# One comparison a tile for both kinds of one-hots, and attention's denominators turned, guarded on GpSimd and spread by a product

## The chip, the cores and the metric

One core of a Trainium2 chip runs the kernel. The metric is the device time of one execution in microseconds (us). Three runs of the kernel before gave 431.22, 433.67 and 428.87 us.

## The reference, cut to what matters

One layer of a graph transformer on 3125 nodes with 256 features. `xn` is the layer norm of x. The graph part sums, for every node, the rows of `xn` over its 53125 edges, adds `w * xn`, and passes the sum through three small products. The mixing part is linear attention over all nodes with 8 heads of 32 features: with q and k after `elu + 1`,

```
k_sum   = k.sum(nodes)                                  # per head, 32 numbers
D_inv   = 1 / maximum(q . k_sum, 1e-6)                  # per node and head
context = k^T v                                         # per head, 32 x 32
attn    = (q @ context) * D_inv
x = x + graph(xn) + attn @ Wproj^T + bproj
x = x + moe(layernorm(x))                               # 8 experts, the best 2 of each token
```

The denominator of one node and head is the product of that node's 32 q features with the head's `k_sum`; its guarded inverse multiplies all 32 features of that head.

## The kernel before, in words

The nodes lie in 25 tiles of 125. The kernel has four stages: projections (q, k, the graph's first product), then the counting stage, which holds all of the change, then routing, then 62 chunks of expert work.

**Counts.** The graph sum is made as a product with a matrix of edge counts. For one tile of 125 nodes, the 625 groups of 5 destination nodes are taken 25 at a time, each with a window of 128 sorted edges on the 128 partitions. VectorE makes two one-hots of every window: `koh` (which of the 125 sources' positions, 126 wide, `key_onehots`, L986) and `loh` (which of 125 places, 128 wide, `local_onehots`, L992), 25 of each, in two instructions of 3150 and 3200 bf16 elements per partition. TensorE multiplies them, 25 products a tile in 7 groups (`count_chunks`, L1366, products at L1381). ScalarE copies each group out (`store_chunks`, L725), two DMA transposes turn the tile's counts (L442, L450), and TensorE multiplies them with the graph's features (`add_up`, L1425, products at L1432, and the node's own term at L1422). Both one-hots are double buffered: VectorE waits for all counts of tile t-2 before it writes those of tile t.

**Attention.** While tile t+1 is counted, tile t is attended to, in a ring over three engines. `denominators(t)` (L1452) multiplies the q features of the tile, as the stationary operand (128 by 125), with `ksum_of` (128 by 8), which gives 125 nodes by 8 heads, in two fp32 products. VectorE (`invert`, L1048) takes the maximum with 1e-6 (L1056) and then the reciprocal (L1057) on 125 by 8. GpSimd (L605) copies each inverse 32 times side by side, to 125 by 256. TensorE (`spread`, L1458) turns that in two transposes (L1463) into features by nodes and runs the next tile's `denominators` right behind. VectorE multiplies with q (`divide`, L1087), TensorE multiplies with the mixing matrix (`attend`, L1475), and VectorE adds the result to x (`mix_add`, L1094).

**Order.** Each engine's program is written out by hand and run in order. TensorE's loop for t = 1 to 24 counts tile t+1 in 7 groups, with `attend(t-1)` after groups 1 and 2, `spread(t)` after group 3 (group 4 for t = 1) and `add_up(t-1)` after group 5. VectorE's loop (L1097) is: both one-hots of t+2, `divide(t)`, `invert(t+1)`, `mix_add(t-1)`; for t = 0 it makes no one-hots and adds nothing, and for t = 1 the one-hots of tile 3 come right behind `invert(1)`. GpSimd has nothing else to do in this stage. SyncE issues the DMA transposes.

**Before the stage.** GpSimd fills constants at the start (L489 to L524). `make_keys` (L955) writes the keys and places that the one-hots are compared with, each doubled, to two separate arrays of 625 by 2.

Of the kernel before, what the change touches and what calls it, by code (L numbers as in the profile page):

```python
# [6 lines left out]
F32, F16, BF16 = mybir.dt.float32, mybir.dt.float16, mybir.dt.bfloat16  # L7
# [17 lines left out]
EPS = 1e-5  # L25
MAGIC = 12582912.0
CB = 2 * TP
ROW = D + 6
# [36 lines left out]
def build(nc, a, out):  # L65
# [4 lines left out]
    with ExitStack() as ctx:  # L70
# [45 lines left out]
        def homes(region, at, n):  # L116
# [18 lines left out]

        r = Region("region_a", GT * (KW + P) + 2 * NT * P + 2)
        koh = r.take(P, 2 * GT * KW, BF16).rearrange("p (s c n) -> p s c n", s=2, c=GT)
        loh = r.take(P, 2 * GT * P, BF16).rearrange("p (s c n) -> p s c n", s=2, c=GT)
        adj = [r.take(P, NT * P, BF16).rearrange("p (t n) -> p t n", t=NT) for _ in range(2)]
        r.take(P, 2)  # L140
        adjT_at = r.at
# [8 lines left out]
        assert r.at <= adjT_at + NT * P  # L150
        r.restart(adjT_at - 2 - NT * P // 2)
        eq = r.take(P, 4 * TP).rearrange("p (s n) -> p s n", s=2)
        rq = r.take(P, 4 * TP).rearrange("p (s n) -> p s n", s=2)
        assert r.at <= adjT_at - 2
        r.restart()
# [100 lines left out]
        spill = sb("spill", [P, 1], I32)  # L256
        keys = sb("keys", [P, NG, 2], BF16)
        locs = sb("locs", [P, NG, 2], BF16)

# [3 lines left out]
        ksum_of = sb("ksum_of", [P, 2, NH])  # L263
        den = sb("den", [TP, 2, 2 * NH])
        wide = sb("wide", [TP, 2, D])
        qn = sb("qn", [P, 2, 2 * TP])
# [50 lines left out]
            "value_done", "held_done", "held_ready", "turned", "keys_done", "spill_known"))  # L317
        pad_zeroed, wident_done, koh_done, loh_done, chunk_ready, adj_done = map(sem, (
            "pad_zeroed", "wident_done", "koh_done", "loh_done", "chunk_ready", "adj_done"))
# [3 lines left out]
        den_ready, den_inv, widened, den_spread, qn_done, mix_ready, mix_added = map(sem, (  # L323
            "den_ready", "den_inv", "widened", "den_spread", "qn_done", "mix_ready", "mix_added"))
        spill_copied, spill_landed, spill_step, spill_ready, spill_summed = map(sem, (
# [162 lines left out]
        def _(pool):  # L488
# [34 lines left out]
            nc.gpsimd.tensor_copy(ident16[:], ident[:]).then_inc(pool_set, 1)  # L523
            nc.gpsimd.memset(adj[0][:, :, TP:P], 0.0).then_inc(pad_zeroed, 1)  # L524

            def set_tables():
# [73 lines left out]
            for t in range(NT):  # L600
                pool.wait_ge(den_inv, t + 1)
                if t >= 2:
                    pool.wait_ge(den_spread, t - 1)
                heads = den[:, 1, t % 2 * NH:(t % 2 + 1) * NH].rearrange("p (h a) -> p h a", a=1)
# [248 lines left out]
        def _(dve):  # L853
# [101 lines left out]
            def make_keys(second):  # L955
                if not second:
# [9 lines left out]
                link(nc.vector.tensor_scalar(keyf[:, lo:hi], keyf[:, lo:hi], MAGIC, -MAGIC, ALU.add, ALU.add))  # L966
                twice = keyf[:, lo:hi].rearrange("p (n a) -> p n a", a=1).to_broadcast([P, n, 2])
                nc.vector.scalar_tensor_tensor(
                    locs[:, lo:hi, :], twice, -float(P),
                    got.rearrange("p (n a) -> p n a", a=1).to_broadcast([P, n, 2]), ALU.mult, ALU.add)  # L970
                nc.vector.tensor_scalar(keys[:, lo:hi, :], twice, unheld[:, 0:1], None, ALU.add
                                        ).then_inc(keys_done, 1)
# [5 lines left out]

            def columns(v, t, n):
                return v[:, t * GT:(t + 1) * GT, :].rearrange("p c (a u) -> p c a u", a=1).to_broadcast(  # L980
                    [P, GT, n // 2, 2])

            def counting(n):
                return iota16[:, 0:n].rearrange("p (a m u) -> p a m u", a=1, u=2).to_broadcast([P, GT, n // 2, 2])

            def key_onehots(t):  # L986
                if t >= 2:
                    dve.wait_ge(chunk_ready, NBLK * (t - 1))
                nc.vector.tensor_tensor(koh[:, t % 2, :, :].rearrange("p c (m u) -> p c m u", u=2), counting(KW),  # L989
                                        columns(keys, t, KW), ALU.is_equal).then_inc(koh_done, 1)  # L990

            def local_onehots(t):  # L992
                if t >= 2:
                    dve.wait_ge(chunk_ready, NBLK * (t - 1))
                nc.vector.tensor_tensor(loh[:, t % 2, :, :].rearrange("p c (m u) -> p c m u", u=2), counting(P),  # L995
                                        columns(locs, t, P), ALU.is_equal).then_inc(loh_done, 1)

            link(moments(0, J, 0))
# [5 lines left out]
            for t in range(NT):  # L1004
# [32 lines left out]
                if t in (17, 18):  # L1037
                    make_keys(t == 18)
                if t == 19:
                    key_onehots(0)  # L1040
                if t == 20:
                    local_onehots(0)
                if t == 21:
                    key_onehots(1)
                if t == 22:
                    local_onehots(1)

            def invert(t):  # L1048
                if t == 0:
                    dve.wait_ge(den_ready, 1)  # L1050
                else:
                    dve.wait_ge(den_spread, t)
                if t >= 2:
                    dve.wait_ge(widened, t - 1)
                heads = slice(t % 2 * NH, (t % 2 + 1) * NH)
# [16 lines left out]
            last.then_inc(ksum_done, 1)  # L1072
            key_onehots(2)
# [3 lines left out]
            local_onehots(2)  # L1077
            dve.wait_ge(heads_ready, 1)
# [235 lines left out]
        def _(pe):  # L1314
# [51 lines left out]
            def count_chunks(n):  # L1366
                t, i = divmod(n, NBLK)
                lo, hi = BLOCKS[i]
                if i == 0:
                    pe.wait_ge(koh_done, t + 1)  # L1370
                    pe.wait_ge(loh_done, t + 1)
                if n == 0:
                    pe.wait_ge(keys_done, 2)
                elif n < NBLK:
                    pe.wait_ge(adj_done, n)
                elif n > 2 * NBLK:
                    pe.wait_ge(adj_done, n - 2)
                elif n > NBLK:
                    pe.wait_ge(adj_done, n - 1)
                for c in range(lo, hi):  # L1380
                    last = nc.tensor.matmul(count_bank(n)[:, (c - lo) * TP:(c - lo + 1) * TP], loh[:, t % 2, c, :],  # L1381
                                            koh[:, t % 2, c, 0:TP], start=True, stop=True)
                last.then_inc(chunk_ready, 1)
# [352 lines left out]
```

## Time and profile before

| | |
|---|---|
| runs | 428.87, 431.22, 433.67 us |
| profiled execution, its own time | 430.48 us |
| its span, first to last instruction | 428.8 us |
| mean granted TensorE clock, share of full speed | 0.962 |
| TensorE busy with products | 404.5 us, 94% |
| VectorE busy | 311.2 us, 73% |
| ScalarE busy | 265.8 us, 62% |
| GpSimd busy | 183.5 us, 43% |

The 1.68 us between the span and the execution's own time lie around the first and the last instruction. PE is TensorE's products and PEld its weight loads, DVE is VectorE, ACT ScalarE, POOL GpSimd, and SPq SyncE's queue of DMAs. Busy shares are means over four stages with different limits; the counting stage is the stretch from about 97 to 220 us. An fp32 product stands in the trace as two passes, and a row says "x4" for two products. The chain of waits is the work that ended last, followed back from the end; each piece is counted from the end of the piece before it, so its pieces can be added, while the durations in the timeline include latency and overlap.

### The profile page before, as it was taken

The numbers are of one execution on the slowest core, as the hardware profiler recorded it, in microseconds if no ns is written. First come the engines' busy times: TensorE is split into PE (matmuls) and PEld (weight loads), VectorE is DVE, ScalarE is ACT, GpSimd is POOL, SyncE is SP. The second block draws the span as 40 slices with busy tenths as digits, with TensorE's granted clock in tenths as the row PEclk, the third lists the DMA queues.
The fourth block names the chain that finished last, engine by engine and source line by source line (L and its number), as shares of the span: only waits on it lengthen the run. The fifth ranks groups of instructions, "written<-read, shape, count | busy, mean of one in ns | idle before, by whom it ended". The sixth has DMA issues, their size and how long they took to land.

```text
span 428.8 us, 10052 instructions
## 1 busy us (share of the span) xinstructions
PE 404.5 (94%) x3141; PEld 318.8 (74%) x3141; DVE 311.2 (73%) x785; ACT 265.8 (62%) x676; POOL 183.5 (43%) x298
## 2 busy tenths in 40 slices
PE   4989899997999999999999999978999999999995
PEld 1767678776677777777755667854999998988894
DVE  3688858967899999999727653667688887655553
ACT  1756655575788888888824614441776766666663
POOL 4058969246100010001091114464456565655655
PEclk9899999999999999999999987577999999999999
DMA  8927310006589999999997961124465665467651
GB/s 211 194 70 255 90 26 8 1 2 125 106 152 172 172 175 167 179 184 189 167 215 227 308 224 63 65 81 120 151 190 188 187 210 159 140 202 207 186 177 38
DMA packets 111827, 64.11 MB, mean 150 GB/s; under 512 B 87985, under 2 KB 102202, under 8 KB 111646
## 3 DMA queue, kind: packets, MB, share of 16 engines
q1 hardware_dynamic: 104590, 48.14, 51.0%
q0 software_dynamic: 6368, 14.47, 9.6%
q10 hardware_dynamic: 816, 0.85, 0.8%
q8 instruction: 26, 0.43, 0.4%
q14 instruction: 27, 0.22, 0.2%
HBM read 24.00 MB, written 21.44 MB: 106 GB/s over the span
## 4 chain that ended last, share of the span: by engine, by line
PE 52%; POOL 12%; issue 11%; DMA 10%; DVE 10%; ACT 3%; SPq 1%; POOLq 0%; DVEq 0%
PE bank L1432 9%; PE bank L1381 8%; PE bank L1475 6%; POOL xs_next L653 5%; PE bank L1346 4%; PE bank L1444 4%; DMA region_a<-xs_next 4%; PE bank L1355 3%; POOL out L660 3%; DMA out<-region_a 3%; PE bank L1612 2%; PE bank L1594 2%; PE bank L1454 2%; DMA xs_next<-region_a 2%; POOL region_a L648 2%
## 5 line engine op out<-in xcount | busy, mean ns | idle before, releaser
L725 ACT CAST region_a<-bank 128x500 bf16<-128x500 f32 (+1 forms) x119 | 70.0, 673 | 14.8 <-PE bank L1381 14.8
L1681 PE MATMUL bank<-region_a,region_c 128*128 128x128 f32 x496 | 65.6, 275 | 0.0
L1692 PE MATMUL bank<-region_c,region_a 128*128 128x256 f32 x248 | 64.0, 380 | 0.0
L1681 PEld LDWEIGHTS bank<-region_a,region_c 128*128 128x128 f32 x496 | 60.3, 191 | 0.1
L1142 DVE COPY region_c<-region_w 128x1026 f32 x62 | 43.5, 701 | 19.2 <-issue 17.7
L605 POOL COPY wide<-den 125x256 f32<-125x256 f32 x25 | 13.0, 518 | 100.6 <-DVE den L1057 100.6
L1381 PE MATMUL bank<-region_a 128*128 128x125 bf16 x625 | 52.9, 219 | 1.5 <-ACT region_a L725 1.4
L1381 PEld LDWEIGHTS bank<-region_a 128*128 128x128 bf16 x625 | 42.2, 101 | 13.6 <-ACT region_a L725 3.2
L989 DVE TENSOR_TENSOR region_a<-iota,keys 128x3150 bf16<-128x3150 bf16 x25 | 44.9, 1796 | 5.4 <-PE bank L1381 5.4
L1304 DVE SCALAR_TENSOR_TENSOR region_a<-bank,region_a 128x256 f32<-128x256 f32 x62 | 30.0, 484 | 22.1 <-PE bank L1692 19.9
L815 ACT COPY region_a<-bank 128x256 f32<-128x256 f32 x62 | 23.1, 373 | 36.9 <-PE bank L1670 36.8
L995 DVE TENSOR_TENSOR region_a<-iota,locs 128x3200 bf16<-128x3200 bf16 x25 | 45.9, 1835 | 0.0
L1692 PEld LDWEIGHTS bank<-region_c,region_a 128*128 128x128 f32 x248 | 42.3, 191 | 3.7 <-ACT region_a L823 0.3
L653 POOL DMA_INDIRECT xs_next<-region_a x31 | 31.0, 999 | 29.1 <-POOL region_a L648 22.9
L634 POOL DMA_INDIRECT xs<-rows,slot_i x25 | 24.7, 987 | 43.8 <-ACT rows L769 28.3
L1432 PE MATMUL bank<-region_a,region_z 125*64 125x500 bf16 (+1 forms) x375 | 40.7, 347 | 0.0
L660 POOL DMA_INDIRECT out<-region_a x31 | 30.6, 986 | 23.1 <-POOL region_a L648 15.5
L823 ACT ACTIVATE region_a<-bank,region_c 128x128 f32<-128x128 f32 x124 | 38.5, 362 | 0.0
L725 ACT CAST region_w<-bank 128x500 bf16<-128x500 f32 (+1 forms) x56 | 32.4, 667 | 9.0 <-PE bank L1381 9.0
L1432 PEld LDWEIGHTS bank<-region_a,region_z 125*64 125x64 bf16 x375 | 21.8, 109 | 17.4 <-DMA region_a<-region_w 0.2
L834 ACT COPY bank<-region_q 128x256 f32 x62 | 23.4, 377 | 18.3 <-DVE region_a L1304 16.4
L1346 PE MATMUL bank<-region_p,region_a 128*125 128x320 f32 x100 | 32.2, 445 | 0.0
(239 smaller groups left out, 775.6 us busy)
## 6 DMA issues: line engine op xcount, KB each, us to landing
region_a<-xs_next SPq DMA_DIRECT2D x31, 259.0 KB, 2.9
region_w<-in_w SPq DMA_DIRECT2D x4, 1024.0 KB, 9.7
region_a<-xs SPq DMA_DIRECT2D x31, 131.0 KB, 2.4
rows<-in_x SPq DMA_DIRECT2D x5, 560.0 KB
xs_next<-null SPq DMA_DIRECT2D x8, 259.0 KB, 4.9
xs_next<-null SPq DMA_DIRECT2D x1, 1554.0 KB, 11.4
xs<-null SPq DMA_DIRECT2D x8, 131.0 KB, 3.1
region_q<-in_b SPq DMA_DIRECT2D x1, 1024.0 KB, 9.6
```

Source lines behind the costliest of these rows:

```text
L653: nc.gpsimd.indirect_dma_start(xs_next, bass.IndirectOffsetOnAxis(to_row[:, c:c + 1], 0), xch[:, c % XB, :], None, bounds_check=RR - 1, oo ...
L660: nc.gpsimd.indirect_dma_start(out, bass.IndirectOffsetOnAxis(to_row[:, c:c + 1], 0), xch[:, c % XB, PART:WIDE], None, bounds_check=N - 1, ...
L725: nc.scalar.copy(to, count_bank(n)[:, 0:w * TP].rearrange("p (c t u) -> p c t u", c=w, t=NT)).then_inc(adj_done, 1)
L823: last = nc.scalar.activation(hT[:, c % 2, f * P:(f + 1) * P], hid_ps[c % 2][:, f * P:(f + 1) * P], ACT.Gelu, bias=wc[:, c % 3, 4 * D + f: ...
L989: nc.vector.tensor_tensor(koh[:, t % 2, :, :].rearrange("p c (m u) -> p c m u", u=2), counting(KW), columns(keys, t, KW), ALU.is_equal).th ...
L995: nc.vector.tensor_tensor(loh[:, t % 2, :, :].rearrange("p c (m u) -> p c m u", u=2), counting(P), columns(locs, t, P), ALU.is_equal).then ...
L1142: nc.vector.tensor_copy(wc[:, c % 3, :].rearrange("p (a f) -> p a f", a=1), w_all[:, bass.ds(e, 1), :]).then_inc(w_copied, 1)
L1346: last = nc.tensor.matmul((y0, y1)[s][0:TP, 0:H1 + D], xnT[:, s, k, :], wzkv[:, k, 0:H1 + D], start=(k == 0), stop=(k == 1))
L1381: last = nc.tensor.matmul(count_bank(n)[:, (c - lo) * TP:(c - lo + 1) * TP], loh[:, t % 2, c, :], koh[:, t % 2, c, 0:TP], start=True, stop ...
L1432: last = nc.tensor.matmul(sum_out(lo, hi - lo), zparts[:, t, part, :], adjT[0:TP, t % 2, lo:hi, 0:TP], start=False, stop=False, skip_group ...
L1681: last = nc.tensor.matmul(hid_ps[c % 2][:, f * P:(f + 1) * P], wc[:, c % 3, k * D + f * P:k * D + (f + 1) * P], xT[:, c % 2, k * P:(k + 1) ...
L1692: last = nc.tensor.matmul(y_ps[c % 2][:, 0:D], hT[:, c % 2, f * P:(f + 1) * P], wc[:, c % 3, (2 + f) * D:(3 + f) * D], start=False, stop=( ...
```

## The change

VectorE makes both one-hots of a tile with one instruction of 6300 elements: the array `onehots` holds them as kinds 0 and 1, each in rows of 128, of which 126 are written; the last two columns of kind 1 are set to zero once, as VectorE's first instruction. Tiles 0 to 2 keep two instructions, one for each kind. The keys and places stand interleaved by tile in `pairs`, so one operand reaches both.

The denominators of a tile come out as 8 heads by 125 nodes: `ksum_of` is now the stationary operand and q the moving one. VectorE takes the reciprocal straight from PSUM, 8 partitions by 125 elements. GpSimd applies the guard as a minimum with 1e6 on the same shape. A product with `head_of` (8 by 256, one where the feature belongs to the head) spreads the inverse over the features, in place of the copy and the two transposes. `head_of` is made by GpSimd at the start with a memset and two selects.

```diff
+        onehots = r.take(P, 4 * GT * P, BF16).rearrange("p (s k c n) -> p s k c n", s=2, k=2, c=GT)
-        den_ps = h0[0:TP, CB:CB + NH]
+        den_ps = h0[0:NH, CB:CB + TP]
...
+            nc.gpsimd.memset(head_of[:], 1.0).then_inc(pool_set, 1)
+            nc.gpsimd.affine_select(out=head_of[:], ...)          # twice
...
-                pool.wait_ge(den_inv, t + 1)
+                pool.wait_ge(inverted, t + 1)
                 if t >= 2:
                     pool.wait_ge(den_spread, t - 1)
-                nc.gpsimd.tensor_copy(wide[:, t % 2, :].rearrange("p (h a) -> p h a", a=HD),
-                                      heads.to_broadcast([TP, NH, HD])).then_inc(widened, 1)
+                nc.gpsimd.tensor_scalar(den[:, 1, t % 2, :], den[:, 0, t % 2, :], 1.0 / DEN_MIN, None, ALU.min
+                                        ).then_inc(den_inv, 1)
...
-            def key_onehots(t): ...
-            def local_onehots(t): ...
+            def make_onehots(t, kinds):
+                if t >= 2:
+                    dve.wait_ge(chunk_ready, NBLK * (t - 1))
+                n = len(kinds) * GT
+                kinds = slice(kinds[0], kinds[-1] + 1)
+                return nc.vector.tensor_tensor(
+                    onehots[:, t % 2, kinds, :, 0:KW].rearrange("p k c (m u) -> p (k c) m u", u=2),
+                    iota16[:, 0:KW].rearrange("p (a m u) -> p a m u", a=1, u=2).to_broadcast([P, n, KW // 2, 2]),
+                    pairs[:, t, kinds, :, :].rearrange("p k c (a u) -> p (k c) a u", a=1).to_broadcast([P, n, KW // 2, 2]),
+                    ALU.is_equal)
+            nc.vector.memset(onehots[:, :, 1, :, KW:P], 0.0)
...
             def invert(t):
...
-                link(nc.vector.tensor_scalar(den[:, 0, heads], den_ps, 1e-6, None, ALU.max))
-                nc.vector.reciprocal(den[:, 1, heads], den[:, 0, heads]).then_inc(den_inv, 1)
+                nc.vector.reciprocal(den[:, 0, t % 2, :], den_ps).then_inc(inverted, 1)
...
                 if 1 <= t < NT - 2:
-                    key_onehots(t + 2)
-                    local_onehots(t + 2)
+                    make_onehots(t + 2, (0, 1)).then_inc(onehots_done, 1)
...
             def denominators(t):
                 for c in range(2):
-                    last = nc.tensor.matmul(den_ps[:, 0:NH], qp_all[:, t, c * TP:(c + 1) * TP], ksum_of[:, c, :],
+                    last = nc.tensor.matmul(den_ps, ksum_of[:, c, :], qp_all[:, t, c * TP:(c + 1) * TP],
                                             start=(c == 0), stop=(c == 1))
             def spread(t):
-                pe.wait_ge(widened, t + 1)
+                pe.wait_ge(den_inv, t + 1)
...
-                    last = nc.tensor.transpose(spread_ps[:, c * TP:(c + 1) * TP], wide[:, t % 2, c * P:(c + 1) * P],
-                                               ident[0:TP, 0:TP])
+                    last = nc.tensor.matmul(spread_ps[:, c * TP:(c + 1) * TP], head_of[:, c * P:(c + 1) * P],
+                                            den[:, 1, t % 2, :], start=True, stop=True)
```

## Rows read from the trace of the kernel before

**Rows 1.** Busy us, 150 to 180: TensorE, loads, VectorE, ScalarE, GpSimd; clock, DMA, GB/s.
```profile
150.00:180.00 30.00, 30.00 (x338) 22.83 (x335) 28.23 (x42) 25.32 (x46) 2.80 (x7) 1.00 1.05 180
```

**Rows 2.** Chain of waits, whole run: start, us, what; `add_up` of four tiles.
```profile
115.69 1.56 PE bank L1432 x15
...
149.58 1.45 PE bank L1432 x13
...
191.85 1.56 PE bank L1432 x15
...
215.00 1.56 PE bank L1432 x15
```

**Rows 3.** Chain of waits, one tile from 157.9 us: what TensorE does in turn.
```profile
157.91 0.22 PE bank L1463 x2
158.13 0.34 PE bank L1454 x4
...
160.54 0.62 PE bank L1381 x9
...
161.65 0.23 PE bank L1381 x4
```

**Rows 4.** Chain of waits, projections: eight fp32 passes of 125 columns.
```profile
51.39 0.90 PE bank L1355 x8
```

**Rows 5.** Timeline of one tile: start, us, engine, line, shapes, idle before.
```profile
156.06 1.80 DVE L989 TENSOR_TENSOR region_a<-iota,keys 128x3150 bf16<-128x3150 bf16 x1 [0.22 <-PE bank L1381]
...
157.78 1.82 DVE L995 TENSOR_TENSOR region_a<-iota,locs 128x3200 bf16<-128x3200 bf16 x1
...
159.51 0.41 DVE L1087 TENSOR_TENSOR qn<-bank,region_q 128x250 f32<-128x250 f32 x1
159.84 0.16 DVE L1056 TENSOR_SCALAR den<-bank 125x8 f32<-125x8 f32 x1
...
160.04 0.20 DVE L1057 RECIPROCAL den<-den 125x8 f32<-125x8 f32 x1
...
160.30 0.40 POOL L605 COPY wide<-den 125x256 f32<-125x256 f32 x1 [4.28 <-DVE den L1057]
...
160.74 1.80 DVE L989 TENSOR_TENSOR region_a<-iota,keys 128x3150 bf16<-128x3150 bf16 x1 [0.22 <-PE bank L1381]
...
162.42 0.39 PE L1463 MATMUL bank<-ident,wide 125*128 125x125 f32 x2
```

**Rows 6.** VectorE's groups by shape: busy us, mean ns, idle; two widths of reciprocal.
```profile
L873 DVE RECIPROCAL rstd<-std 125x10 f32<-125x10 f32 x2 | 0.4, 214 | 0.0
...
L1180 DVE RECIPROCAL rstd<-std 125x3 f32<-125x3 f32 x2 | 0.4, 176 | 0.4 <-ACT std L766 0.4
```

**Rows 7.** Timeline of the stage's start, 102 to 109 us: the ring's first two rounds.
```profile
102.68 0.15 DVE L1056 TENSOR_SCALAR den<-bank 125x8 f32<-125x8 f32 x1
...
102.98 1.77 DVE L995 TENSOR_TENSOR region_a<-iota,locs 128x3200 bf16<-128x3200 bf16 x1
103.13 1.89 POOL L605 COPY wide<-den 125x256 f32<-125x256 f32 x1 [0.89 <-DVE den L1057]
...
105.88 0.42 DVE L1087 TENSOR_TENSOR qn<-bank,region_q 128x250 f32<-128x250 f32 x1 [0.72 <-PE bank L1454]
...
106.67 1.86 POOL L605 COPY wide<-den 125x256 f32<-125x256 f32 x1 [1.66 <-DVE den L1057]
...
108.19 2.02 DVE L995 TENSOR_TENSOR region_a<-iota,locs 128x3200 bf16<-128x3200 bf16 x1
...
108.58 0.43 PE L1463 MATMUL bank<-ident,wide 125*128 125x125 f32 x2 [0.67 <-POOL wide L605]
```

**Rows 8.** Timeline of the kernel's start: first instructions after the constants.
```profile
6.49 1.73 DVE L865 BATCH_NORM_STATS2 stats<-rows 125x6 f32<-125x256 f32 x5 [6.49 <-DMA rows<-in_x]
...
10.14 1.36 POOL L552 TENSOR_SCALAR rows<-rows,rstd,shift 125x256 f32<-125x256 f32 x2 [5.18 <-DVE region_a L882]
```

**Rows 9.** VectorE's groups by shape: the keys of four fifths of the tiles.
```profile
L971 DVE TENSOR_SCALAR keys<-region_c,unheld 128x1000 bf16<-128x1000 f32 x1 | 0.7, 735 | 0.0
```

More of the change, by code:

```diff
@@ L26 @@
 MAGIC = 12582912.0
+DEN_MIN = 1e-6
 CB = 2 * TP
@@ L134, in build @@
         zr = sb("zr", [TP, J, H1])[:]
-        r = Region("region_a", GT * (KW + P) + 2 * NT * P + 2)
-        koh = r.take(P, 2 * GT * KW, BF16).rearrange("p (s c n) -> p s c n", s=2, c=GT)
-        loh = r.take(P, 2 * GT * P, BF16).rearrange("p (s c n) -> p s c n", s=2, c=GT)
+        r = Region("region_a", 2 * GT * P + 2 * NT * P)
+        onehots = r.take(P, 4 * GT * P, BF16).rearrange("p (s k c n) -> p s k c n", s=2, k=2, c=GT)
         adj = [r.take(P, NT * P, BF16).rearrange("p (t n) -> p t n", t=NT) for _ in range(2)]
-        r.take(P, 2)
         adjT_at = r.at
@@ L256, in build @@
         spill = sb("spill", [P, 1], I32)
-        keys = sb("keys", [P, NG, 2], BF16)
-        locs = sb("locs", [P, NG, 2], BF16)
+        pairs = sb("pairs", [P, NB * 5, 2, GT, 2], BF16)
+        keys, locs = pairs[:, :, 0, :, :], pairs[:, :, 1, :, :]
         mout = sb("mout", [P, 2, D])
@@ L263, in build @@
         ksum_of = sb("ksum_of", [P, 2, NH])
-        den = sb("den", [TP, 2, 2 * NH])
-        wide = sb("wide", [TP, 2, D])
+        den = sb("den", [NH, 2, 2, TP])
+        head_of = sb("head_of", [NH, D])
         qn = sb("qn", [P, 2, 2 * TP])
@@ L524, in _ @@
             nc.gpsimd.memset(adj[0][:, :, TP:P], 0.0).then_inc(pad_zeroed, 1)
+            nc.gpsimd.memset(head_of[:], 1.0).then_inc(pool_set, 1)
+            pool.wait_ge(pool_set, 3)
+            nc.gpsimd.affine_select(out=head_of[:], in_=head_of[:], compare_op=ALU.is_ge, fill=0.0, base=0,
+                                    pattern=[[1, D]], channel_multiplier=-HD).then_inc(pool_set, 1)
+            pool.wait_ge(pool_set, 4)
+            nc.gpsimd.affine_select(out=head_of[:], in_=head_of[:], compare_op=ALU.is_ge, fill=0.0, base=HD - 1,
+                                    pattern=[[-1, D]], channel_multiplier=HD).then_inc(pool_set, 1)
             def set_tables():
@@ L966, in make_keys @@
                 link(nc.vector.tensor_scalar(keyf[:, lo:hi], keyf[:, lo:hi], MAGIC, -MAGIC, ALU.add, ALU.add))
-                twice = keyf[:, lo:hi].rearrange("p (n a) -> p n a", a=1).to_broadcast([P, n, 2])
+                tiles = slice(lo // GT, hi // GT)
+                by_tile = "p (t c a) -> p t c a"
+                twice = keyf[:, lo:hi].rearrange(by_tile, c=GT, a=1).to_broadcast([P, n // GT, GT, 2])
                 nc.vector.scalar_tensor_tensor(
-                    locs[:, lo:hi, :], twice, -float(P),
-                    got.rearrange("p (n a) -> p n a", a=1).to_broadcast([P, n, 2]), ALU.mult, ALU.add)
-                nc.vector.tensor_scalar(keys[:, lo:hi, :], twice, unheld[:, 0:1], None, ALU.add
+                    locs[:, tiles, :, :], twice, -float(P),
+                    got.rearrange(by_tile, c=GT, a=1).to_broadcast([P, n // GT, GT, 2]), ALU.mult, ALU.add)
+                nc.vector.tensor_scalar(keys[:, tiles, :, :], twice, unheld[:, 0:1], None, ALU.add
                                         ).then_inc(keys_done, 1)
@@ L977, in make_keys @@
                                             ).then_inc(wident_done, 1)
[L979 to L986, printed above, removed]
+            def make_onehots(t, kinds):
                 if t >= 2:
                     dve.wait_ge(chunk_ready, NBLK * (t - 1))
[L989 to L996, printed above, removed]
+                n = len(kinds) * GT
[6 more added lines that the diff above has]
+            nc.vector.memset(onehots[:, :, 1, :, KW:P], 0.0)
             link(moments(0, J, 0))
@@ L1038, in _ @@
                     make_keys(t == 18)
[L1039 to L1046, printed above, removed]
+                if t in (19, 21):
+                    make_onehots((t - 19) // 2, (0,))
+                if t in (20, 22):
+                    make_onehots((t - 20) // 2, (1,)).then_inc(onehots_done, 1)
             def invert(t):
@@ L1053, in invert @@
                 if t >= 2:
-                    dve.wait_ge(widened, t - 1)
-                heads = slice(t % 2 * NH, (t % 2 + 1) * NH)
-                link(nc.vector.tensor_scalar(den[:, 0, heads], den_ps, 1e-6, None, ALU.max))
-                nc.vector.reciprocal(den[:, 1, heads], den[:, 0, heads]).then_inc(den_inv, 1)
+                    dve.wait_ge(den_inv, t - 1)
+                nc.vector.reciprocal(den[:, 0, t % 2, :], den_ps).then_inc(inverted, 1)
             dve.wait_ge(ctx_ready, 1)
@@ L1072, in _ @@
             last.then_inc(ksum_done, 1)
-            key_onehots(2)
+            make_onehots(2, (0,))
             dve.wait_ge(ctx_turned, 1)
@@ L1076, in _ @@
             invert(0)
-            local_onehots(2)
+            make_onehots(2, (1,)).then_inc(onehots_done, 1)
             dve.wait_ge(heads_ready, 1)
@@ L1380, in count_chunks @@
                 for c in range(lo, hi):
-                    last = nc.tensor.matmul(count_bank(n)[:, (c - lo) * TP:(c - lo + 1) * TP], loh[:, t % 2, c, :],
-                                            koh[:, t % 2, c, 0:TP], start=True, stop=True)
+                    last = nc.tensor.matmul(count_bank(n)[:, (c - lo) * TP:(c - lo + 1) * TP], onehots[:, t % 2, 1, c, :],
+                                            onehots[:, t % 2, 0, c, 0:TP], start=True, stop=True)
                 last.then_inc(chunk_ready, 1)
```

16 lines of the change are left out of this document (7 added, 9 removed).

## The prediction

> **What bounds the kernel now.** I read the busy times by stretch first. In the counting stage TensorE is busy for all of 30 us at full granted clock, VectorE for 28.2 of them [rows 1]. Busy products alone prove nothing, so the chain of waits comes next: there the same product line returns tile after tile, and its distance changes with TensorE's work and with nothing else. Seven tiles in a row take (149.58 - 115.69)/7 = 4.84 us, five later ones (215.00 - 191.85)/5 = 4.63 us [rows 2]. The first seven run the node's own fp32 product by itself, the last five have none. A loop that another engine paced would not notice. Over all 21 tiles between the first and the last row the mean is 99.31/21 = 4.73 us. Third, the timeline of one tile: VectorE goes round in 3.45 us of one-hots (156.06 to 159.51), 0.33 to the maximum, 0.20 to the reciprocal and 0.48 to the end of the addition, 4.46 us, and then stands 0.22 us idle until TensorE has finished a count [rows 5]. So TensorE sets the pace and VectorE follows closely. What the change saves on VectorE and GpSimd is worth nothing until TensorE is shorter; what it adds to TensorE is paid every tile.
>
> **TensorE, every tile.** Before, the two transposes take 0.22 us and the two denominator products 0.34 us, 0.56 in all [rows 3]. The transposes are one pass each, and the denominators pass only 8 columns. After, both are full fp32 products with 125 moving columns: two for `spread`, two for the denominators, eight passes. The nearest row is the projection of q, also fp32, 125 columns and 128-column weights: eight passes in 0.90 us, 0.11 each [rows 4]. The bounds: at the price of a bf16 count of 125 columns, 0.23/4 = 0.058 us [rows 3], eight passes cost 0.46, a gain of 0.10; from above, 0.11 plus a change of array shape, priced below. I take 0.90, the row with the same type and width: **+0.34 us a tile**. The pace becomes 4.97 to 5.18 us, 5.07 in the mean. Rounds 2 to 24 of `spread` and the 22 denominators behind them pay it: 22 x 0.34 + (0.45 - 0.22) = **+7.7 us**.
>
> **VectorE, every tile.** The merged one-hots take between 3.30 us (3.45 less one small instruction, 0.15) and the old 3.45; I take 3.40, since nearly all elements remain. The maximum and its wait, 0.20, go. The reciprocal grows from 8 columns to 125, on fewer partitions. No row shows that width. Three columns take 176 ns and ten take 214 [rows 6], 5.4 ns a column, so 125 take 0.214 + 115 x 0.0054 = 0.84 us. From below the bound is the present 0.20 us; from above a price with no fixed part, 0.20/8 x 125 = 3.1 us, which the seven columns for 38 ns speak against. The round is then 3.40 + 0.33 + 0.84 + 0.28 = 4.85 us. That is 0.39 longer than now, yet hidden under TensorE's 4.97; the cover is only 0.12 us.
>
> **GpSimd, every tile.** The minimum covers 125 elements where the copy wrote 256 in 0.40 us; I take 0.3, between 0.15 and 0.40. It starts 0.06 us behind the reciprocal, beside the addition, and has until the next one-hots: 0.28 us of addition and 0.12 or more of idle time. TensorE asks for it 1.68 us after the one-hots begin [rows 5]. Hidden.
>
> **The stage's start, once.** Here the ring is bare, and GpSimd's copy runs beside one-hots: it takes 1.89 and 1.86 us in place of 0.40, and comes out 0.26 us after the one-hot instruction that began just before it [rows 7]. The Trainium skill's "SBUF — State Buffer" (the part on engine ports) says the pair of ports that the two engines share is locked for a whole instruction; the two rows agree. In the second round the copy slips out between the two one-hot instructions. Merged, there is no gap. Step by step:
> - Reciprocal from 102.68 to 103.52, one-hots until 105.21, guard out 105.47 (the copy: 105.02).
> - `spread(0)`, then `divide(0)`: 0.86 us after the copy before, now 1.20 with the 0.34, so 106.67 (105.88 before).
> - Reciprocal 107.00 to 107.84; merged one-hots 107.76 to 111.21; guard out 111.47. The copy was out at 108.53, and TensorE had already been waiting 0.67 us for it: 2.94 us late, all of it idle.
> - `spread(1)` with its products: 0.34 more.
>
> **+3.3 us.** In the third round `mix_add` waits for TensorE, and the guard slips in. Bounds: with a reciprocal of 0.20 and eight passes at 0.46, the same steps give +1.1; with a reciprocal of 1.15, +3.9.
>
> **What costs nothing.** The Vector queue's new memset stands ahead of statistics that wait 6.49 us for x; GpSimd's memset and two selects fall into 5.18 us of waiting before its first row scaling [rows 8]. The keys are written in another arrangement with as many elements; one such instruction takes 0.735 us [rows 9], and I take 0 for it, with 0.7 as the upper end. No DMA is added or moved.
>
> **Sum.** 430.48 + 7.7 + 3.3 = **441.5 us**. The profiled execution is 0.7 under the median of the runs shown, so against that median the same sum would be 442.2; I forecast 441.5, and 437 to 445 as this case's own range.
>
> **Rivals.**
> - *VectorE becomes the pace.* From a reciprocal of 0.96 us on, its round is longer than TensorE's shortest tile. With a slope half as steep again as the row's, 8.1 ns, it takes 0.214 + 115 x 0.0081 = 1.15 us and the round 5.16: 21 x 5.16 - 99.31 = 9.1, plus 3.9 at the start and 0.6 for the last rounds, **444.1 us**. Against it: the slope of rows 6. For it: the cover is 0.12 us. 
> - *The array's shape is changed more often.* Behind the 64-column products, nine counts take 0.62 us, while nine at 0.058 are 0.52 [rows 3]: a change costs about 0.10. Operands 8 wide could add two changes a tile, 23 x 0.20 = 4.6: **446.1 us**. The Trainium skill's "TensorEngine Tiling (Array Packing)" (key properties) says that a change of tiling mode drains the engine; whether 8 rows or 8 columns make one, no row shows.
> - *The guard is shut out by the one-hots in the steady state.* If GpSimd loses the 0.4 us window, it comes out some 0.2 after 3.45 us of one-hots, and TensorE, which asks at 1.68, stands 2.0 us. VectorE then idles behind TensorE and the next guard slips through, so every second tile pays: 11 x 2.0 on top, **463.5 us**. It decides once the guard has not begun when the addition ends. Against it: at 108.19 the one-hots were stretched to 2.02 us while GpSimd finished [rows 7], so the engine that begins first keeps its turn.
> - *Narrow operands make fp32 passes cheap, and it is not slower.* If a pass with 8 rows or 8 columns in use costs what a bf16 count of 125 columns does, 0.058 us, each tile gains 0.10: -2.3 us, and the start costs 2.4: **430.6 us**. Break-even for the tile is 0.07 a pass. Against it: the q projection at 0.11, and the own product, whose two passes make 4.84 of 4.63, 0.11 each, with half of the columns [rows 2, 4]. To be clearly faster it would also need the start to cost nothing.
>
> **How the numbers follow.** Chances: forecast 0.58, VectorE 0.15, array shape 0.10, shut-out 0.04, not slower 0.13, of which 0.04 falls below -1%. A measurement of this kernel can tell about 1%, 4.3 us, from no change. All cases but the last are slower by more than that, less 0.01 for a forecast that comes out small: slower 0.86, same 0.10, faster 0.04. The range takes in the forecast with its bounds (start +1.1, keys 0.7, passes), VectorE and array shape: 435 to 449 us, 0.83 of the chance.
>
> **What would show it.** TensorE still without idle time between 120 and 210 us, `add_up` returning every 5.07 us, and the two products together at 0.9 us in the chain: right. A reciprocal near 0.84 us, and VectorE idle before the one-hots by 0.1 to 0.3 us: the cover held. TensorE idle in every tile, released by the one-hots, is the first rival; by GpSimd's guard in every second tile, the third. TensorE waiting some 3 us at `spread(1)` shows the start. If passes with 8 rows take under 0.07 us, the prediction is wrong at its main term.

## The result, and the profile after

The kernel after takes **452.64 us** (median of 4 runs, 450.94 to 456.70) against 430.38 for the kernel before, a ratio of **1.0532** [1.0485, 1.0579]. Slower was right; 441.5 was not, nor the range to 449. The profiled execution takes 453.56 us with a span of 451.8, so it stands 23.08 above that of before.

First, where in the span it lies: the chain of waits of the kernel after (start, us, what). L1455 is `spread`, L1446 `denominators`, L1373 the counts, L1424 `add_up`.

```profile
112.72 1.22 PE bank L1455 x4
...
115.40 2.95 PE bank L1424 x15
...
124.20 1.56 PE bank L1424 x15
...
160.95 0.63 PE bank L1455 x4
161.58 0.53 PE bank L1446 x4
162.11 0.55 PE bank L1373 x8
162.65 1.45 PE bank L1424 x13
...
164.26 0.60 PE bank L1373 x9
...
165.35 0.22 PE bank L1373 x4
...
167.98 1.45 PE bank L1424 x13
...
237.15 1.56 PE bank L1424 x15
...
239.21 6.40 DMA region_a<-region_a
...
245.65 1.63 PE bank L1424 x15
```

`add_up(1)`, at 115.69 before, starts at 124.20: **+8.5 us**. One tile's price is in this number, since `spread(2)` and its products stand ahead of `add_up(1)` in TensorE's program. From there to `add_up(22)`, 21 tiles take 237.15 - 124.20 = 112.95 us, where they took 99.31 [rows 2]: **+13.6**, or 5.38 us a tile for 4.73. The last `add_up` of the kernel before, in its chain:

```profile
222.40 1.44 PE bank L1432 x15
```

From `add_up(22)` to there the last two rounds took 7.40 us, now 8.50: **+1.1**; 0.4 of it is the last `spread`, the rest TensorE's wait for a DMA transpose at the end. Behind that nothing is lost: 451.8 - 245.65 = 206.15 us against 428.8 - 222.40 = 206.4. The three terms make 23.2.

Inside a tile, against [rows 3]: `spread` 0.63 for 0.22, `denominators` 0.53 for 0.34, and the eight counts behind them 0.55, where eight at the 0.058 of [rows 3] are 0.46. That is 0.41 + 0.19 + 0.09 = 0.69. The other counts are slightly cheaper (0.60 for 0.62, 0.22 for 0.23), and the distance from `add_up` to `add_up` grows from 4.68 to 5.33, by 0.65.

Is TensorE still the pace? The windows of the kernel after (stretch: busy us and count of TensorE, loads, VectorE, ScalarE, GpSimd; granted clock, DMA share, GB/s):

```profile
104.00:105.00 1.00, 0.02 (x1) 0.00 (x0) 1.00 (x1) 0.00 (x0) 1.00 (x1) 1.00 0.05 11
105.00:106.00 1.00, 0.24 (x2) 0.24 (x3) 0.70 (x3) 0.00 (x0) 0.70 (x1) 1.00 1.10 213
106.00:108.00 2.00, 2.00 (x12) 1.22 (x12) 0.26 (x1) 0.00 (x0) 0.00 (x0) 0.50 1.13 216
...
118.00:119.00 1.00, 1.00 (x9) 0.68 (x7) 0.00 (x0) 0.00 (x0) 0.00 (x0) 0.50 0.00 0
...
120.00:122.00 2.00, 1.83 (x18) 1.39 (x17) 1.67 (x2) 1.45 (x3) 0.00 (x0) 1.00 0.81 154
...
150.00:180.00 30.00, 30.00 (x303) 20.99 (x303) 27.45 (x24) 22.00 (x39) 2.75 (x6) 1.00 0.93 159
```

From 150 to 180 us TensorE is busy throughout, as in [rows 1], and VectorE less than before. The upper rows show what the forecast had no term for: TensorE is nearly idle from 104 to 106 us, and the granted clock then stands at 0.50, its level of 1.2 GHz, until 119 us. In the kernel before TensorE is busy for 0.93 us between 104 and 106, and the clock stays at 1.00.

The timeline of the kernel after for one tile and for the second round of the start (start, us, engine, line, shapes, idle time before):

```profile
103.75 1.95 POOL L610 TENSOR_SCALAR den<-den 8x125 f32<-8x125 f32 x1 [1.45 <-DVE den L1051]
...
105.76 1.02 PE L1455 MATMUL bank<-den,head_of 8*128 8x125 f32 x4 [1.74 <-POOL den L610]
...
108.93 3.36 DVE L991 TENSOR_TENSOR region_a<-iota,pairs 128x6300 bf16<-128x6300 bf16 x1
109.09 3.58 POOL L610 TENSOR_SCALAR den<-den 8x125 f32<-8x125 f32 x1 [3.39 <-DVE den L1051]
...
162.82 0.92 DVE L1051 RECIPROCAL den<-bank 8x125 f32<-8x125 f32 x1
...
163.83 0.51 POOL L610 TENSOR_SCALAR den<-den 8x125 f32<-8x125 f32 x1 [4.99 <-DVE den L1051]
...
164.46 3.44 DVE L991 TENSOR_TENSOR region_a<-iota,pairs 128x6300 bf16<-128x6300 bf16 x1 [0.45 <-PE bank L1373]
```

TensorE waits 1.74 us for the first guard. In the steady state VectorE waits 0.45 us for TensorE, and the guard finishes within the addition and that wait. At the start the guard stands beside the merged one-hots for 3.58 us and comes out 0.38 us behind them.

### The profile page after: what moved, and what is told of

It is laid out like the page before. It is cut to its first block, busy times and chain, and to the rows that moved or that the text cites. A ratio compares the mean times of both kernels' runs of the same rounds, so it can differ in the third digit from the quotient of the medians.

```text
span 451.8 us, 10105 instructions
## 1 busy us (share of the span) xinstructions
PE 422.6 (94%) x3187; PEld 324.4 (72%) x3191; DVE 322.6 (71%) x739; ACT 265.3 (59%) x676; POOL 189.2 (42%) x301
## 4 chain that ended last, share of the span: by engine, by line
PE 54%; DVE 21%; DMA 8%; issue 7%; ACT 4%; SPq 2%; DVEq 2%; POOL 2%; POOLq 0%; ACTq 0%
PE bank L1424 8%; PE bank L1373 8%; PE bank L1467 5%; DVE region_c L1135 4%; PE bank L1339 4%; PE bank L1455 3%; PE bank L1436 3%; PE bank L1673 3%; PE bank L1684 3%; PE bank L1446 3%; PE bank L1348 3%; DVE region_a L1297 3%; PE bank L1604 2%; DVE region_a L1291 2%; DMA out<-region_a 2%
## 5 line engine op out<-in xcount | busy, mean ns | idle before, releaser
L991 DVE TENSOR_TENSOR region_a<-iota,pairs 128x6300 bf16<-128x6300 bf16 (+1 forms) x28 | 86.5, 3090 | 10.0 <-PE bank L1373 10.0
L730 ACT CAST region_a<-bank 128x500 bf16<-128x500 f32 (+1 forms) x119 | 69.0, 662 | 25.8 <-PE bank L1373 25.7
L610 POOL TENSOR_SCALAR den<-den 8x125 f32<-8x125 f32 x25 | 17.3, 692 | 118.9 <-DVE den L1051 118.9
L1373 PE MATMUL bank<-region_a 128*128 128x125 bf16 x625 | 53.5, 222 | 1.4 <-ACT region_a L730 1.4
L1373 PEld LDWEIGHTS bank<-region_a 128*128 128x128 bf16 x625 | 40.3, 99 | 19.5 <-ACT region_a L730 6.3
L1297 DVE SCALAR_TENSOR_TENSOR region_a<-bank,region_a 128x256 f32<-128x256 f32 x62 | 30.0, 484 | 23.2 <-PE bank L1684 20.7
L820 ACT COPY region_a<-bank 128x256 f32<-128x256 f32 x62 | 23.2, 374 | 37.5 <-PE bank L1662 37.2
L1424 PE MATMUL bank<-region_a,region_z 125*64 125x500 bf16 (+1 forms) x375 | 42.1, 356 | 0.7 <-DMA region_a<-region_a 0.7
L1424 PEld LDWEIGHTS bank<-region_a,region_z 125*64 125x64 bf16 x375 | 22.2, 112 | 19.3 <-issue 1.6
L1467 PE MATMUL bank<-mout,qn 128*125 128x256 f32 x100 | 32.2, 409 | 0.2 <-DVE rows L1088 0.2
```

The lines of the kernel that those rows point to most:

```text
L730: nc.scalar.copy(to, count_bank(n)[:, 0:w * TP].rearrange("p (c t u) -> p c t u", c=w, t=NT)).then_inc(adj_done, 1)
L991: return nc.vector.tensor_tensor(onehots[:, t % 2, kinds, :, 0:KW].rearrange("p k c (m u) -> p (k c) m u", u=2), iota16[:, 0:KW].rearrange ...
L1297: nc.vector.scalar_tensor_tensor(xch[:, s, PART:WIDE], y_ps[c % 2][:, 0:D], xch[:, s, weight:weight + 1], xch[:, s, PART:WIDE], ALU.mult, ...
L1424: last = nc.tensor.matmul(sum_out(lo, hi - lo), zparts[:, t, part, :], adjT[0:TP, t % 2, lo:hi, 0:TP], start=False, stop=False, skip_group ...
L1467: last = nc.tensor.matmul(mix_ps[0:TP, 0:D], qn[:, t % 2, c * TP:(c + 1) * TP], mout[:, c, :], start=(c == 0), stop=(c == 1))
```

## The experiments

Theory A: the narrow operands cost TensorE a price at each change of shape, and the start costs a late guard and the clock that falls. Rivals: narrow fp32 passes are slower in themselves; VectorE or GpSimd sets the pace. Changes stand against the kernel after unless said otherwise. Ratios are against the kernel before. "Start" is the place of `add_up(1)`, less the shift of the whole stage in that execution (read at the copy of `mout`, 102.08 us before and 102.13 after). Outside the counting stage the profiled executions differ also between kernels that are the same there: in the fourteen profiles the copy of `mout` starts between 102.03 and 105.01 us, and from the last `add_up` to the end 203.1 to 208.7 us pass, with the granted clock below 1.00 for a part of that in every one. So a step is priced inside the stage, and medians of four runs tell small steps less well.

**1. Full width for both products.**

```diff
-        den = sb("den", [NH, 2, 2, TP])
-        head_of = sb("head_of", [NH, D])
-        ksum_of = sb("ksum_of", [P, 2, NH])
+        den = sb("den", [P, 2, 2, TP])          # rows from 8 on are zero
+        head_of = sb("head_of", [P, D])         # as above
+        ksum_of = sb("ksum_of", [P, 2, P])      # columns from 8 on are zero
...
```

> The changed kernel with both narrow operands filled up with zeros: head_of and the guarded inverses on 128 rows in place of 8, ksum_of 128 columns in place of 8. The same products, the same number of moving columns. Theory A (operands 8 wide cost extra, by a change of the array's shape): spread falls from 0.64 to about 0.45 us, denominators from 0.53 to about 0.45, the counts behind them from 0.55 to 0.47: the pace falls by 0.25 to 0.35 us a tile to about 5.0 to 5.05, 446 to 448 us. Theory B (fp32 products in this place cost what they cost, whatever their width): pace unchanged at 5.3 to 5.5, 452 to 453 us.

444.69 us, 1.0324 [1.0243, 1.0405], a little below what was expected. The chain of this kernel, its first and last of 22 `add_up` and one tile (the lines stand one further down than after):

```profile
122.28 1.56 PE bank L1425 x15
...
162.10 0.50 PE bank L1456 x4
162.60 0.45 PE bank L1447 x4
163.05 0.44 PE bank L1374 x8
...
228.49 1.56 PE bank L1425 x15
```

The same eight passes with sixteen times the rows or columns are **cheaper**: 0.13, 0.08 and 0.11 us less, 0.32 a tile. The 21 tiles take 106.21 us, 5.06 each; the forecast's pace was 5.07. The +0.34 was thus the price of full-width operands, and the change doesn't have these.

**2. Full width for `spread` alone** (the first two lines above).

> The changed kernel with only the spreading product filled up, 128 rows in place of 8; the denominators keep their 8 columns. Theory A: spread 0.64 to about 0.45 us, denominators stay 0.53; pace 5.1 to 5.15, 448 to 450 us. Theory B: nothing moves, 452 to 453 us. If the extra sits in the change between the two shapes and not in either product, it comes out between the two or shifts to the denominators.

448.92 us, 1.0416 [1.0334, 1.0499]. The chain:

```profile
165.08 0.50 PE bank L1456 x4
165.58 0.53 PE bank L1447 x4
166.11 0.55 PE bank L1374 x8
```

One excess goes, that of `spread`; those of the denominators and of the counts stay.

**3 and 4. Each pair of narrow products issued twice**, `spread`'s or the denominators', into the same place.

```diff
-                    last = nc.tensor.matmul(spread_ps[...], head_of[...], den[...], start=True, stop=True)
+                    for _ in range(2):
+                        last = nc.tensor.matmul(spread_ps[...], head_of[...], den[...], start=True, stop=True)
```

> The kernel after with the two products of spread issued twice, one pair behind the other, into the same place. It tells the two halves of the narrow operands' price apart. Theory A (a fixed price of about 0.10 us each time the products change their shape: full to 8 rows, 8 rows to 8 columns, 8 columns to full): the repeated pair changes no shape once it has begun, since its weights alternate between two 8-row blocks, so it costs the full-width price of four passes, 0.45 to 0.50 us a tile; pace 5.33 to 5.80, time 452.6 + 22 x 0.47 = 463. Theory B (an fp32 pass with 8 rows is itself slower, 0.16 us in place of 0.11): the repeated pair costs 0.63 a tile; pace 5.96, time 466.5.

> The kernel after with the two denominator products issued twice. Theory A (a fixed price at each change of shape): the repeated pair costs 0.42 to 0.46 us a tile, the pace goes from 5.33 to about 5.77 and the time to about 462. Theory B (a pass into 8 columns is itself slower): 0.53 a tile, pace 5.86, time 464.

460.72 us (1.0756 [1.0720, 1.0792]) and 462.58 us (1.0779 [1.0742, 1.0816]). The chain with `spread` twice:

```profile
162.74 1.08 PE bank L1456 x8
163.82 0.52 PE bank L1446 x4
```

The chain with the denominators twice (L1449 are the repeated ones):

```profile
165.11 0.63 PE bank L1458 x4
165.74 0.53 PE bank L1446 x4
166.27 0.43 PE bank L1449 x4
```

The second `spread` costs 1.08 - 0.63 = 0.45 us and the second denominators 0.43: four passes at 0.11, the price of [rows 4]. Narrow passes are therefore not slower in themselves; what costs is the first group after each change, from full to 8 rows, to 8 columns, and back to full. That settles it for the rival "slow passes". With `spread` twice the time came out 2 us below the expectation; the start of its profiled execution is 0.9 us earlier than after's, which is a part of that.

**5. The guard on VectorE instead of GpSimd.**

```diff
-                nc.gpsimd.tensor_scalar(den[:, 1, t % 2, :], den[:, 0, t % 2, :], 1.0 / DEN_MIN, None, ALU.min)
+                nc.vector.tensor_scalar(den[:, 1, t % 2, :], den[:, 0, t % 2, :], 1.0 / DEN_MIN, None, ALU.min)
...                                         # the waits move with it
```

> The changed kernel with the guard (the minimum on 8 by 125) on VectorE, right behind the reciprocal, in place of GpSimd. Theory: in the steady tiles nothing moves, since VectorE idles 0.45 us a tile and the guard costs it about 0.2: pace stays 5.33 to 5.49 us. At the start the guard no longer waits out one-hots (1.95 and 3.58 us on GpSimd), spread(1) comes 3 to 5 us earlier, TensorE has no long idle time and the granted clock stays at 2.4 GHz: 6 to 8 us less, 444.5 to 447 us. Rival (the start's delay is the wider products and the reciprocal, not GpSimd's wait): less than 2 us, over 450.5 us. Rival 2 (VectorE is the hidden pace): the pace grows by 0.2 us a tile, 4 us lost again.

448.12 us, 1.0412 [1.0351, 1.0473], above the expectation. The chain of this kernel, first three `add_up`:

```profile
109.24 1.56 PE bank L1421 x15
...
116.00 1.56 PE bank L1421 x15
...
121.49 1.56 PE bank L1421 x15
```

The pace is unchanged (5.49 us here, 5.33 later). The start is back at 116.00 (115.69 before), and the clock stays at 1.00 in it: nearly the whole +8.5 hangs on the guard's place on GpSimd. By the medians that is worth 4.5 us, not 8.2; this profiled execution spends 2 us more than after's behind the stage, at work that the edit leaves alone.

**6. The clock held at the start:** products of zeros keep TensorE busy where it waited.

```diff
+            filler(8)                # 8 products of zeros, added to a bank of sums
             spread(0)
...
+                    if t == 1 and i == 4:
+                        filler(11)
```

> The changed kernel with 8 products of zeros in front of spread(0) and 11 in front of spread(1), 512 columns each, added to a bank that is being summed, so TensorE is busy where it waited for GpSimd. Theory C (the start costs 8.5 us, of which some 4 to 6 because the granted clock falls to 1.2 GHz from 106 to 119 us): the clock stays at 2.4 GHz there, and the time falls by 4 to 6 us to 447 to 449; add_up of tile 1 comes at about 119 to 120 in place of 124.2 us. Rival D (the late guard alone makes the start, the clock is beside the point): the clock stays up and the time falls by less than 1.5 us. Rival E: products of zeros don't keep the clock, nothing changes.

450.57 us, 1.0484 [1.0392, 1.0576], less gained than expected. The windows of this kernel:

```profile
106.00:108.00 2.00, 1.99 (x13) 1.02 (x12) 0.74 (x3) 0.00 (x0) 0.74 (x1) 1.00 1.11 213
...
114.00:116.00 2.00, 2.00 (x23) 1.10 (x21) 1.26 (x2) 0.72 (x1) 0.35 (x1) 1.00 0.00 0
```

and its chain, the second guard and the first two `add_up`:

```profile
109.41 3.59 POOL den L610
...
114.60 1.56 PE bank L1424 x15
...
121.36 1.56 PE bank L1424 x15
```

The clock stays at 1.00. `add_up(1)` starts at 121.36, in an execution whose stage began 1.09 us later than before (`mout` at 103.17): +4.6. So of the +8.5 in after's profile 3.9 us are the clock. By the medians it is 2.1, whose interval takes in zero. In the other kernels that keep the late guard, the stretch at half clock has other lengths (about 109 to 112 us with the denominators twice), so one execution's 3.9 us is no constant.

**7. Full width and the guard on VectorE** (1 and 5 together): what is left, and who sets the pace.

> Both narrow operands filled up to the whole array and the guard on VectorE: the best mended form of the changed ring. TensorE's work is 5.0 us a tile; VectorE's is about 4.9 plus the guard's 0.2. Theory: VectorE now sets the pace at 5.05 to 5.15 us, TensorE waits 0.05 to 0.15 us a tile for one-hots, the start is 6 us shorter than in the changed kernel: 437 to 441 us, still 1.5 to 2.5% over the kernel before, since spread and denominators cost 0.95 us against 0.56. Rival (the two repairs don't add, because the start's clock was already better with the filled operands): 442 to 444 us.

441.02 us, 1.0205 [1.0133, 1.0277]. Its windows:

```profile
150.00:180.00 30.00, 30.00 (x320) 23.05 (x318) 29.80 (x31) 23.39 (x43) 0.00 (x0) 1.00 0.95 165
```

and its timeline of VectorE:

```profile
158.88 3.42 DVE L988 TENSOR_TENSOR region_a<-iota,pairs 128x6300 bf16<-128x6300 bf16 x1
...
163.99 3.42 DVE L988 TENSOR_TENSOR region_a<-iota,pairs 128x6300 bf16<-128x6300 bf16 x1
```

and one row of its chain, `attend` behind the nine counts:

```profile
159.18 0.58 PE bank L1465 x2
```

From about 150 us on VectorE sets the pace: these rows show no wait of VectorE, and its one-hots return every 5.1 us, where TensorE's tile in run 1 takes 5.01 in this part. TensorE's wait shows in `attend`, which needs VectorE's addition of the tile before and takes 0.58 us here, 0.49 in run 1. In the seven tiles ahead of that both runs take 5.17 us, so there TensorE still sets it. TensorE reads 30.00 in the window, so its busy share alone would have named the wrong engine, as the prediction said of busy products. The start is as before (`add_up(1)` at 115.66). The rival "VectorE becomes the pace" is true of this kernel's later tiles and not of the kernel after, where the narrow products lengthened TensorE's tile past VectorE's round.

**8 and 9. The merged one-hots alone**, with the old ring: in every tile, and in every tile but the third.

```diff
+                    if t == 1:                        # run 9 only
+                        make_onehots(3, (0,))
+                        make_onehots(3, (1,))
+                    else:
                     make_onehots(t + 2, (0, 1))
```

> The changed kernel with attention's ring as it was before (maximum, copy on GpSimd, two transposes, 8-column denominators); only the merged one-hots stay. My theory (TensorE sets the pace, its two wider products are the steady loss): the pace goes back to 4.6 to 4.85 us a tile, VectorE idles about 0.3 us a tile, and only the start stays dearer by 1.2 to 1.7 us, since GpSimd's second copy waits out one long one-hot instruction: 431 to 433 us, ratio 1.000 to 1.006. Rival (the merged instruction carries a steady loss of its own, by keeping GpSimd out): over 436 us, with TensorE waiting for GpSimd in the steady tiles.

> The old ring with merged one-hots, except that tile 3 keeps two instructions, so that GpSimd's second copy slips in between. Theory: the 2 to 5 us that the merged one-hots alone lost are the start's (spread(1) 1.6 us later, and a longer idle time of TensorE in which its clock can fall); they go, and the pace of 4.59 to 4.80 us, 0.04 below that of before, leaves 429 to 430.5 us, ratio 0.997 to 1.002. Rival (the loss is spread over the stage or lies behind it): 432 to 435 us as with all tiles merged.

434.90 us (1.0097 [1.0054, 1.0140]), more than expected, and 429.96 us (0.9987 [0.9956, 1.0018]), as expected. In both the 21 tiles take 98.46 us for 99.31, 0.04 us less a tile and 0.85 in all, which the second can't tell from nothing. In the first, GpSimd's copy takes 3.50 us beside the merged instruction of tile 3, and `add_up(1)` comes at 117.27, +1.6; in the second it slips in between the two instructions in 1.86 us, as in [rows 7]. The first kernel's 5 us are more than these rows hold: its last `add_up` is only 0.7 us later than before's. Of the 2.8 us by which its profile is longer, 2.1 lie behind the stage, within the spread told above.

**10. The rest of run 8's loss: the clock?** Run 8 with 11 products of zeros ahead of `spread(1)`.

> The ring of before with the merged one-hots in every tile, and 11 products of zeros on TensorE ahead of spread(1), where it otherwise stands idle for some 2 us. If the part of the loss of 4 to 5 us that the profiled execution does not show is a fall of the clock after that idle time, this comes out near 431, 3 to 4 us under the kernel without the products of zeros (434.9). If it is not the clock, the time stays at 433.5 to 436.

431.10 us, 1.0049 [1.0020, 1.0078]. The median is the one expected of the clock, but the intervals of the two runs overlap, and the windows don't bear the reason out. Run 8, without the products of zeros:

```profile
104.00:106.00 2.00, 0.96 (x13) 0.97 (x14) 1.27 (x4) 0.00 (x0) 0.98 (x1) 1.00 0.72 139
...
108.00:110.00 2.00, 0.00 (x0) 0.00 (x0) 1.88 (x1) 1.64 (x3) 2.00 (x1) 1.00 0.30 57
```

Run 10, with them:

```profile
104.00:106.00 2.00, 0.92 (x11) 0.83 (x11) 1.27 (x4) 0.00 (x0) 1.11 (x1) 0.99 0.66 127
106.00:108.00 2.00, 2.00 (x15) 1.82 (x13) 1.97 (x4) 1.69 (x3) 1.23 (x1) 0.50 1.11 213
```

Run 8 kept its clock through 2 us of idle time, and run 10 lost it after a pause that run 8 has as well. In run 10's profile the products of zeros end late and bring the last `add_up` 1.6 us later than in run 8; what its profile gains, 3.2 us, lies behind the stage (205.3 us for 208.5), where the edit changes nothing. Whether the medians' difference has the same source, and what else the merged third tile costs, stays open.

**11 and 12. The turned ring alone**, one-hots in two instructions throughout; and the same with a copy on GpSimd in place of the minimum.

```diff
-                    make_onehots(t + 2, (0, 1))
+                    make_onehots(t + 2, (0,))
+                    make_onehots(t + 2, (1,))
...
-                nc.gpsimd.tensor_scalar(den[:, 1, t % 2, :], den[:, 0, t % 2, :], 1.0 / DEN_MIN, None, ALU.min)
+                nc.gpsimd.tensor_copy(den[:, 1, t % 2, :], den[:, 0, t % 2, :])      # run 12 only
```

> The changed kernel with two one-hot instructions a tile throughout, in the new layout; the turned ring stays. Theory: the steady pace stays 5.3 to 5.5 us (VectorE loses 0.05 to 0.1 of its 0.45 us of idle time), at the start GpSimd's second guard slips in between the two instructions, 1.7 us earlier: 449.5 to 452 us. So the turned ring alone explains 19 to 21 of the 22 us. Rival (merging is what costs): under 446 us.

> The turned ring with two one-hot instructions throughout (as in the run that does the attention part alone), and on GpSimd a copy of the 8 by 125 inverses in the place of the minimum, so the guard is left out. In the ring of before a copy of 125 by 256 slips in between the two one-hot instructions of tile 3 (1.86 us); the minimum of 8 by 125 did not (3.64 us). If the kind of operation decides, the second copy takes about 1.9 us here and the start loses some 1.7 us less; time about 450. If its shape or its moment decides, it takes 3.6 us again and the time stays at 452. The steady pace is 5.33 by both.

452.40 us (1.0492 [1.0424, 1.0560], 0.4 above the expected range) and 451.00 us (1.0504 [1.0443, 1.0564]). The turned ring alone makes the whole loss; the steady pace is after's in both. The split did not help the guard of run 11. The timeline of run 11:

```profile
111.78 3.43 DVE L991 TENSOR_TENSOR region_a<-iota,pairs 128x3150 bf16<-128x3150 bf16 x2
111.95 3.64 POOL L610 TENSOR_SCALAR den<-den 8x125 f32<-8x125 f32 x1 [3.58 <-DVE den L1051]
```

and of run 12:

```profile
109.85 3.42 DVE L991 TENSOR_TENSOR region_a<-iota,pairs 128x3150 bf16<-128x3150 bf16 x2
109.98 3.44 POOL L610 COPY den<-den 8x125 f32<-8x125 f32 x1 [2.64 <-DVE den L1051]
```

The time can't tell the two expectations apart, but the duration does: a copy of 8 by 125 waits out both instructions too, so the kind of operation doesn't decide. Its shape or its moment does, and which of them was not tried.

## Why the prediction was wrong, step by step

The step that failed is "TensorE, every tile": it forecast +0.34 us, and the runs showed +0.65, because the sum put three changes of operand shape, 0.32 us a tile, at nothing. The start failed too: its sum had no term for the granted clock.

| step | forecast, us | measured, us | by |
|---|---|---|---|
| `spread` and denominators, rounds 2 to 24 | +7.7 | 0.65 + 13.6 + 0.4 = +14.7 | chain; runs 1 to 4 |
| the stage's start, without round 2 | +3.3 | 8.5 - 0.65 = +7.8 | chain; runs 5, 6 |
| DMA transpose at the end | 0 | +0.7 | chain; runs 3, 4, 6 have none |
| VectorE, GpSimd in the steady state | 0 | 0 | VectorE idle 0.45 |
| keys, memsets, behind the stage | 0 | -0.25, within the spread there | chain |

- **What bounds it:** right. TensorE paced the stage before and after, and what VectorE saved gave nothing.
- **TensorE's tile, +0.34:** the passes were sized rightly, as operands of full width show (5.06 us a tile for 5.07 forecast). Left out of the sum were the changes of shape: three a tile, 0.32 us in all, about 0.11 each, measured as 0.13, 0.08 and 0.11. The rival "the array's shape is changed more often" had them, with two changes at 0.10 where there are three: one into 8 rows, one from these to 8 columns, one back. With 0.32 the rival's 23 x 0.20 = 4.6 becomes 7.4, and the forecast 441.5 + 7.4 = 448.9. The row that told it was in hand: nine counts at 0.62 for 0.52 behind the 64-column products [rows 3] were read as the price of a change and then given a chance of 0.10. The Trainium skill's "TensorEngine Tiling (Array Packing)" (key properties) says that a change of tiling mode drains the engine. The 0.08 to 0.13 us at each change fit that, if 8 rows and 8 columns make such modes; no run shows the drain itself.
- **VectorE hidden:** right. The reciprocal takes 0.92 us (forecast 0.84, first rival from 0.96 on), the merged one-hots 3.44 (3.40); the cover of 0.12 us became 0.45 only because TensorE's tile was longer. Run 7 shows how thin it was.
- **GpSimd hidden in the steady state:** right, with 0.51 us for 0.3. The rival "shut out" did not occur.
- **The start, +3.3:** the mechanism was right, a guard locked out by the merged one-hots (out at 112.67, forecast 111.47). With the clock held it costs 4.6. Of the 1.3 above the forecast, 0.4 is a guard that comes out at 113.00 - 1.09 = 111.91, and 0.2 are `spread(1)` and its followers (from the guard to `add_up(0)` 1.60 us for 1.07 before, 0.53 more where 0.34 was forecast). The other 0.65 is no cost of the start but round 2's products ahead of `add_up(1)`, which the forecast counted with the tiles. Another 3.9 us in the profiled execution, and 2.1 by the medians, is the clock at 1.2 GHz behind the pause for the first guard, a term that the forecast lacked. That guard is out at 103.75 + 1.95 = 105.70 where the copy was out at 105.02 [rows 7]: a reciprocal of 0.92 us stands ahead of it.
- **The rival "not slower":** wrong. Four narrow passes took 0.43 us at the least, 0.11 each.
- **The range:** it reached 445, and 449 with one rival added at a time. Shape and start were both dear at once, 452.64.

## What to carry to other kernels

In a loop paced by TensorE, count each change to a narrow operand and back (here fp32, 8 rows or 8 columns) as about 0.1 us, and try zero padding to full width first: here it cost no TensorE time and saved 0.32 us a tile. Price a change at the start of a stage, where nothing covers a late result, apart from the steady state, and look there for an idle TensorE and the granted clock behind it. Taking work off an engine that is not the bound gains nothing by itself; here the merged one-hots alone are worth 1 us at best.

## What the runs showed of the hardware that was not expected

- Products with 8 of 128 rows or columns take as long as full ones (0.45 and 0.43 us for four passes that repeat a shape; 0.50 and 0.45 at full width in run 1), and the first group behind a change of shape takes 0.08 to 0.13 us more.
- The reciprocal costs about as much a column at 125 columns as the few narrow rows said: 214 ns at 10 [rows 6] and 922 at 125, so (922 - 214)/115 = 6.2 ns a column, for 5.4 between 3 and 10 columns. The wide one also reads PSUM and fills 8 partitions for 125.
- GpSimd can wait out two VectorE instructions that follow each other closely (3.64 and 3.44 us), where a larger copy got in between them (1.86 us, [rows 7] and run 9). The Trainium skill's "SBUF — State Buffer" (SBUF: two separate sides) has the port locked for one whole instruction; the first two rows show a longer wait, and no run says why.
- A pause of TensorE does not always bring its clock down: 2 us without a product were followed by a clock of 1.00 in run 8, while the kernel after fell to 0.50 behind 2 us with 0.26 of products.
- Counts read from the new array of one-hots (both kinds in rows of 128, where one had 126) take 0.60 us for nine and 0.22 for four (before, 0.62 and 0.23 [rows 3]); with the old ring that is 0.04 us a tile. Which part of the new layout does it was not tried.
